# Latent attention with its feed-forward layer: norm two blocks ahead, half a projection in the steps, the window's edge masked on TensorE

## What is computed

```python
q_c = q @ W_dq                                   # q: the normed x, 512 -> 192
q_nope = (q_c @ W_uq); q_rope = rope(q_c @ W_qr) # 16 heads
kv_c = kv @ W_kvc                                # 512 -> 128
k_nope = kv_c @ W_uk; v = kv_c @ W_uv; k_rope = rope(kv_c @ W_kr)
scores = (q_nope . k_nope + q_rope . k_rope) * scale
good = (k_ids <= seg_id) & (k_ids >= seg_id - 8)
scores = where(good, scores, -1e30)
out = softmax(scores) @ v @ W_o
x = x + out
x = x + (silu(ln(x) @ gate * gate_s) * (ln(x) @ up * up_s)) @ down * down_s
```

## Time and profile before

| | us |
|---|---|
| median of the three runs shown (820.82 to 823.79) | 823.74 |
| the profiled execution | 825.13 |
| its span, first to last instruction | 823.2 |
| PE busy in it | 754.3 |
| DVE busy | 461.5 |
| ACT busy | 408.2 |
| POOL busy | 188.3 |
| mean granted clock of PE | 0.955 |
| setup ends at about | 110.5 |
| heads of block 0 begin at | 188 |
| attention ends and the feed-forward layer begins at | 588 |

### The profile page before, as it was taken

How to read it: one execution, slowest core, us unless ns; L and a number is a source line. 1 busy time by engine, 2 the same in 40 slices (tenths; PEclk the granted TensorE clock), 3 DMA queues, 4 the chain that set the end, 5 groups by cost and what they waited for, 6 DMA issues and landing times.

```text
span 823.2 us, 18851 instructions
## 1 busy us (share of the span) xinstructions
PE 754.3 (92%) x7102; PEld 703.3 (85%) x7102; DVE 461.5 (56%) x984; ACT 408.2 (50%) x899; POOL 188.3 (23%) x325
## 2 busy tenths in 40 slices
PE   4899986889999898889899899889999999999997
PEld 4777875769987798779797799778999999999997
DVE  2988763654577345764367545774685263636342
ACT  4788742564446544574355644575588231323231
POOL 2455523433044210533016130422000000000000
PEclk9999996879999899999999899998999999999999
DMA  8899763344322332033320443109120212111021
GB/s 261 260 304 305 248 163 65 80 112 88 71 59 90 78 80 57 26 110 86 66 65 3 123 86 83 34 5 386 65 66 1 59 40 53 43 48 48 15 67 33
DMA packets 46356, 80.89 MB, mean 98 GB/s; under 512 B 5738, under 2 KB 30234, under 8 KB 46282
## 3 DMA queue, kind: packets, MB, share of 16 engines
q1 hardware_dynamic: 40796, 53.34, 25.0%
q0 software_dynamic: 5488, 26.50, 9.4%
HBM read 56.93 MB, written 11.28 MB: 83 GB/s over the span
## 4 chain that ended last, share of the span: by engine, by line
PE 64%; DVE 8%; SPq 5%; issue 3%; ACT 3%; DMA 2%; POOL 1%; DVEq 0%; ACTq 0%; POOLq 0%
PE ps L1335 17%; PE ps L1037 12%; PE ps L907 9%; PE ps L1367 8%; PE ps L1042 6%; SPq L821 5%; PE ps L167 3%; PE ps L980 2%; DVE score L1151 2%; PE ps L953 1%; DVE prob L1175 1%; DMA key_rows<-kv_table,idx 1%; ACT q_lat L1080 1%; PE ps L766 1%; PE ps L1316 1%
## 5 line engine op out<-in xcount | busy, mean ns | idle before, releaser
L1191 DVE TENSOR_TENSOR o_lo<-q_lat,o_hi 128x320 fp32r<-128x320 f32 x80 | 64.6, 813 | 91.0 <-ACT o_hi L1088 88.8
L1037 PE MATMUL ps<-o_hi,wvo_hi 128*128 128x320 f32 x320 | 97.0, 314 | 1.8 <-ACT o_hi L1088 1.8
L1088 ACT ACTIVATE o_hi<-q_lat 128x320 fp32r<-128x320 f32 x80 | 66.9, 842 | 61.1 <-PE ps L1037 60.0
L1037 PE MATMUL ps<-o_hi,wvo_lo 128*128 128x320 f32 x320 | 95.8, 311 | 0.0
L1419 ACT ACTIVATE silu<-ps,ffn_scale 128x320 f32<-128x320 f32 x55 | 29.0, 527 | 97.5 <-PE ps L1335 97.5
L853 POOL TENSOR_TENSOR rot_c<-gathered,cosq 128x192 f32<-128x192 f32 x40 | 27.3, 683 | 213.6 <-PE ps L917 180.1
L1470 DVE SCALAR_TENSOR_TENSOR hidden<-ps,ffn_scale,silu 128x320 f32<-128x320 f32 x55 | 30.2, 549 | 60.5 <-ACT silu L1419 52.9
L1037 PEld LDWEIGHTS ps<-o_hi,wvo_hi 128*128 128x128 f32 x320 | 60.7, 190 | 2.4 <-ACT o_hi L1088 2.1
L1037 PEld LDWEIGHTS ps<-o_hi,wvo_lo 128*128 128x128 f32 x320 | 60.6, 189 | 0.3
L1042 PE MATMUL ps<-o_lo,wvo_hi 128*128 128x320 f32 x320 | 60.4, 310 | 0.0
L487 PE MATMUL ps<-wkv,ctx_hi 128*128 128x384 f32 x192 | 53.4, 388 | 6.4 <-ACT ctx_hi L350 6.4
(11 more groups left out here) (170 smaller groups left out, 1930.6 us busy)
## 6 DMA issues: line engine op xcount, KB each, us to landing
ctx_raw<-ctxT_dram SPq DMA_DIRECT2D x16, 722.0 KB, 7.8
gathered<-key_rows SPq DMA_DIRECT2D x240, 47.2 KB
head_w<-head_w_dram SPq DMA_DIRECT2D x16, 576.0 KB, 5.2
ffn_raw<-ffn_w_dram POOLq DMA_DIRECT2D x11, 768.0 KB, 12.3
kv_table<-tab POOLq DMA_DIRECT2D x16, 288.0 KB, 6.7
rows<-x_dram SPq DMA_DIRECT2D x5, 640.0 KB, 5.2
residual<-x_dram SPq DMA_DIRECT2D x20, 160.0 KB, 2.4
x_rows<-residual SPq DMA_DIRECT2D x20, 160.0 KB, 2.0
```

The source lines that it names most:

```text
L1037: last = pe.matmul(ps[:, 4 + m, 0:TB], w[wt][:, h, cols], o_hi[h % 2][:, :], start=(h == 0 and n == 0), stop=False, skip_group_check=True)
L1088: act.activation(o_hi[h % 2][:, :], q_lat[:, h % 2, :, h // 2], ACT.Copy).then_inc(oh_ok, 1)
L1191: dve.tensor_tensor(o_lo[h % 2][:, :], q_lat[:, h % 2, :, h // 2], o_hi[h % 2][:, :].bitcast(F32), ALU.subtract).then_inc(ol_ok, 1)
```

## The change

- **Norm two blocks ahead.** The norm of block b + 2 is made while the heads of block b run: DVE's pieces behind heads 2 to 9, PE's transposes after heads 10 to 13 (`norm_heads`), ACT's copies beside them. The norm of block 1 is made in block 0: DVE's pieces in its last queries, PE's transposes in its first steps. The norm of the feed-forward layer's block 0 goes into the heads of blocks 3 and 4. SP loads the rows two blocks ahead.
- **Half of the compression earlier.** The first output of `compress` (m = 0) goes to bank 6 in the first steps: two of its products before the third mask, two before the fourth. ACT copies it twice (`take_compressed`), and PE waits for the second copy before the first values. The second output stays after the last values.
- **The edge mask by PE.** The table `edge` and one POOL operation a block (`mask_block`) make a stationary operand for each step; the mask product now adds both masks. L1155 and `neg_all` are gone, and the scale goes into the exponential.
- **The first two gathers of block 0** are issued at the end of the setup by POOL, once the first eight contexts are stored.
- **The loop** holds blocks 1 and 2; block 3 is written out. SP's part is written out whole.

```diff
-def compress(pe, b, m, w, rowsT, ps, ln, qc_mm):
-    pe.wait_ge(ln.hi_ok, Count(NLT)(b, NLT))
-    for c in range(KC):
+def compress(pe, b, m, cs, w, rowsT, bank, ln, qc_mm):
+    if 0 in cs:
+        pe.wait_ge(ln.hi_ok, Count(NLT)(b, NLT))
+    for c in cs:
...
# setup, POOL
                 turns(pool, rope)
+                pool.wait_ge(index_ok, 1)
+                pool.wait_ge(front_in, 16)
+                for i in range(2):
+                    pool.wait_ge(tab_out[i], 16 * (NB // 4))
...
+                for k in range(2):
+                    pool.indirect_dma_start(
+                        out=win[k][:, :], out_offset=None, in_=table,
+                        in_offset=bass.IndirectOffsetOnAxis(ap=w["idx_all"][:, k:k + 1], axis=0),
+                    ).then_inc(win_in[k], 16)
...
+def attention_blocks(eng, body):
+    body(0)
+    with eng.Fori(1, BLOCKS - 2) as b:
+        body(b)
+    body(BLOCKS - 2)
+    body(BLOCKS - 1)
...
# attention, SP
+            if b < BLOCKS - 1:
+                load_rows(b + 2)
+            if b > 0:
+                res.rest(sp, b - 1)
+                res.start(sp, b)
...
# attention, POOL
+        def mask_block(b, first):
+            if not first:
+                pool.wait_ge(s_mm, c16(b - 1, 16))
+            pool.tensor_tensor(
+                masks[:, :, :].rearrange("p s (x r) -> p s x r", r=HH),
+                w["edge"][:, bass.ds(b * STEPS, STEPS), :].unsqueeze(3).to_broadcast([P, STEPS, SPOTS, HH]),
+                w["other"][:, :].rearrange("p (x r) -> p x r", r=HH).unsqueeze(1)
+                .to_broadcast([P, STEPS, SPOTS, HH]), ALU.add).then_inc(mask_ok, 1)
...
             if first:
+                mask_block(0, True)
                 load_index(0)
-                gather(0, 0)
-                gather(0, 1)
                 pool.wait_ge(lone_in, 32)
                 rotate(0, 0, True)
                 rotate(0, 1, True)
                 gather(0, 2)
+                ln.root(pool, 1)
...
                 gather(b + 1, 1)
-                ln.root(pool, b + 1)
                 gather(b + 1, 2)
+            if third:
+                ln_f.root(pool, 0)
+            elif not last:
+                ln.root(pool, b + 2)
...
# attention, PE
+            mask_and_rope(b, 1)
+            latent(b, 1)
+            turn_keys(b, 3)
+            if first:
+                ln.turn(pe, 1, 2, (6, 7))
+                ln.turn(pe, 1, 3, (6, 7))
+            else:
+                compress_main((0, 1))
+            mask_and_rope(b, 2)
+            latent(b, 2)
             turn_probs(b, 0)
+            compress_main(range(KC) if first else (2, 3))
...
-                for t in tiles_at(s):
-                    if last_block:
-                        ln_f.turn(pe, 0, t, (2, 3))
-                    else:
-                        ln.turn(pe, b + 1, t, (2, 3))
-            if not last_block:
+            if not last:
                 pe.wait_ge(s_red, c16(b, 16))
-                compress(pe, b + 1, 0, w, rowsT, ps, ln, qc_mm)
-                compress(pe, b + 1, 1, w, rowsT, ps, ln, qc_mm)
+                compress(pe, b + 1, 1, range(KC), w, rowsT, ps[:, 1, 0:TB], ln, qc_mm)
...
+                if h in norm_heads:
+                    t = norm_heads.index(h)
+                    if last:
+                        ln_f.turn(pe, 0, t, (2, 3))
+                    elif not third:
+                        ln.turn(pe, b + 2, t, (2, 3))
...
# attention, DVE
-            dve.scalar_tensor_tensor(
-                out=sa[:, :, :].rearrange("p (e g) j -> p e (g j)", e=2),
...
+        norm_after = {2: 0, 3: 1, 4: 2, 5: 3, 6: 4, 8: 5, 9: 6}
...
-                if o in stats:
-                    next_norm(b, last, stats.index(o))
+                if first and o >= 11:
+                    ln.piece(dve, 1, (o - 11) // 2, x_in, loads=1)
...
+                if h in norm_after and third:
+                    ln_f.piece(dve, 0, norm_after[h], ffn_x_in)
+                elif h in norm_after and not last:
+                    ln.piece(dve, b + 2, norm_after[h], x_in, loads=b + 2)
```

More of the change, by code:

```diff
@@ L66 @@
 FAR = -2.0 ** 127
+SPOTS = 2 * (GQ + 1)
 MEANS = WIN
@@ L655, in finish, with build_attention @@
             sp.wait_ge(s, 32 * BLOCKS)
-def build_attention(nc, block, ctx, a, w, ffn, ps, ident, table, x1, rows, rowsT, four, ln, ln_f, sums, qc_mm):
+def build_attention(nc, block, ctx, a, w, ffn, ps, ident, table, x1, rows, rowsT, four, ln, ln_f, sums, qc_mm, win,
+                    win_in, four32):
     def sb(name, shape, dt=F32, stack=ctx):
@@ L784, in _, with load_rows @@
     def _(sp):
-        def body(b, first, last):
-            sp.wait_ge(ln.turned, c4(b, NLT))
-            if not last:
-                sp.dma_start(rows[:, :, :], a["x"][bass.ds((b + 1) * TB, TB), :]
+        def load_rows(k):
+            sp.wait_ge(ln.turned, c4(k - 1, NLT))
+            if k < BLOCKS:
+                sp.dma_start(rows[:, :, :], a["x"][k * TB:(k + 1) * TB, :]
                              .rearrange("(t p) d -> p t d", p=LT)).then_inc(x_in, 16)
@@ L982, in values, with body, compress_main @@
             last.then_inc(av_mm, 1)
-        def body(b, first, last_block):
+        def body(b):
+            first, third, last = place(b)
+            def compress_main(cs):
+                if not last:
+                    compress(pe, b + 1, 0, cs, w, rowsT, ps[:, 6, 0:TB], ln, qc_mm)
             pe.wait_ge(qc_lo_ok, c2(b, 2))
+            if not first and not last:
+                pe.wait_ge(ln.hi_ok, c4(b + 1, NLT))
             for o in range(4):
@@ L1018, in body @@
                 if s == 0:
+                    if not last:
+                        pe.wait_ge(qc_full, c1(b, 1))
                     values(b, s)
@@ L1104, in body @@
                 take_latent_keys(b, s)
+                if first:
+                    for t in range(2 * s - 4, 2 * s - 2):
+                        ln.high(act, 1, t, (6, 7))
             take_probs(b, 0)
@@ L1110, in body @@
                     exps(b, s + AHEAD - 1)
+                if s == 0 and not last:
+                    take_compressed(b + 1)
                 if s and s + AHEAD < STEPS:
```

211 lines of the change are left out of this document (118 added, 93 removed).

## The result

The changed kernel takes **800.96 us** (median; 797.89 to 802.26) beside 823.76 us for the kernel before on the same chip: ratio 0.971 [0.965, 0.977]. On another chip it took 804.43 us, ratio 0.975 [0.971, 0.978]. The forecast was 802.3. Its profiled execution took 802.26 us (span 800.6), that of before 825.13 (span 823.2), so 22.9 us less where the sum said 21.4. But the parts of the sum came out otherwise, and the experiments show that two of its reasons were wrong and cancelled others.

What follows compares the result with a forecast made beforehand. PE, busy for 754 of 823 us, was taken as the bound. Terms for block 0, starts, ends, compression, transposes and loop summed to -21.4 us: profiled 825.1 to 803.7, median 802.3; range 795 to 815.

Steps and rivals of the forecast that it cites:

- End of the steps: End of a block's steps: removed DVE work brings the last values 1.3 us earlier; -3.9 in blocks 1 to 3.
- The chain of the new wait in block 0: First mask waits behind third gather (17.8 us after the first spread), POOL's root, two tiles, copy; 137.4 us.
- The transposes: Four tiles between heads 10 to 13, where PE has no gap: +1.5 us in blocks 0, 1, 2 and 4.
- rival B: Heads: PE idles more before them and stays at half clock into two heads per block; +15, 817 us; chance 0.09.
- Block 0: First block in all -7.9 us: -7.3 up to the last values, -2.1 compression, +1.5 transposes.
- Rival A: The first block doesn't start earlier: gather lands no sooner or the new wait eats it; 809 to 810 us; chance 0.14.
- Starts: Start of a block's steps: -0.6 us over blocks 1 to 3, -0.4 in block 4.
- Mask: L1155, 0.27 us mean, leaves DVE's chain 40 times; gives some 0.25 us at a block's start and end.
- The other half at the start: Start of steps: four early compression products fill PE's waits, two of them hidden; -0.2 us in each of blocks 1 to 3.
- Compression: Last values to first head, half left: gains 2.1, 2.3, 2.7 and 2.4 us; -7.4 in blocks 1 to 3.
- Loop: One of two returns goes: -5.0 us, bounds -4.3 and -5.7, or 0 if the written-out code stalls.

## Why the prediction was right, and where it was not

The time was right to 1.3 us, and the sum of the profile to 1.5. That the sum came so near is luck in part: block 0 and the compression gave less than forecast or gave it for another reason, the starts and the loop gave more. The largest part of the change, the norm two blocks ahead, was never undone by itself. The loop (6.1 us) and DVE's step (4.6) were; most of the rest can be the norm's move, but that is inferred from what is left over. Three steps of the prediction held, as far as the profiles tell. *End of the steps*: -3.9 forecast, -4.0 in the first profile of the changed kernel, -2.1 in the second. *The chain of the new wait in block 0*: 17.8 us forecast from SP's start to the third gather, 17.76 measured; 34.5 us to the last values where 35.5 stood. *The transposes* in the heads: 1.6 to 1.8 us a block where 1.5 stood. Of this the transposes are 1.3, by profiles whose heads start at full clock; the rest is rival B in small: the first head of blocks 0 to 3 ran at a mean clock of 0.67 to 0.81 in this profile, at 1.00 before. Block 4 with all behind it lost 2.3 us: 1.3 as above, and 1.0 since the clock stayed at 0.50 for 5.7 us from its first head on instead of 3.3. In the profiles of four of the experiments it stayed there for about as long as before, and the loss is 1.3.

**Block 0**, -7.9 forecast, -3.2 measured. The step that failed is "the first two gathers now go out right there ... so spreads start between 114.1 and 118.4". The gathers went out there, but SP's small DMAs stand behind the end of the setup, and that waited for their landing: SP started at 120.29. The sum's own words had the trap in them: POOL "then waited for the end of the stage". I asked when the gather lands, and not what the stage's end waits for. Rival A had the right place, with another mechanism.

**Starts**, -1.0 forecast (blocks 1 to 4), -4.6 measured. The step "Mask" took L1155 at its mean of 0.27 us. In the first step of a block it takes 0.59 (block 1 before) or 0.75 (put back), beside POOL's rotations, and `prob` is stretched too. The step back alone costs 3.7 us at the four starts. The step "The other half at the start" called the first two early products "hidden" and expected full clock from them: without them the starts of blocks 1 to 3 are 3.2 us shorter in all, and at full clock too. In blocks 1 to 3, then, the step gave 2.2 us, the products took 3.2, and the stretch still fell by 3.0; the step was never put back without the early products, so the two may not add up, and up to 4 us there have no cause shown. The table in section 1, "Specifications", of "GPSIMD Engine Reference" of the Trainium skill says that POOL's way to SBUF is shared with DVE, with contention where a DVE operation has two SBUF inputs. These rows agree: `prob`, with two inputs, takes 0.98 us beside a rotation and 0.22 without. The forecast cited it and said that it "would not change the sum". It did.

**Compression**, -7.4 forecast, -7.5 measured, and this is the right number for the wrong reason. With the compression undivided the end still falls from 22.8 to 18.3 us over blocks 1 to 3, at a clock of 0.73 to 1.00 from the last values to the first head where it was 0.60 to 0.75. What is left by the move is 1.7 to 3.0 us against the two profiles of the changed kernel (2.7 to 8.1 against the six others), and the starts pay 3.2 for it. The faster end, as far as one profile of each can show it (21.6 us in that of the kernel before with block 3 written out), comes from the rest of the change (the norm's work and transposes gone from the last steps, the mask's step gone). With that step put back the ends are 5.52, 5.52 and 5.40 us, as in the changed kernel on that chip (5.52 three times), which speaks for the norm's; the norm's alone was not run. The step that failed is "with one half left: 1.6 us of values + 4.3 us at half clock", set against an end that was itself taken as fixed. Two of its readings were off as well: block 2's first head was taken from a piece of the chain (376.04 us), while PE's timeline has it at

```profile
375.64 0.55 PE L1037 MATMUL ps<-o_hi,wvo_hi 128*128 128x320 f32 x1
```

So that end is 8.1 us and not 8.5, block 3's 6.5 and not 6.9, and the term by its own working is -6.6.

**Loop**, -5.0 forecast, -8.8 measured. The one return taken away gave 6.4 us in the profiles, -6.1 us by itself; the forecast had valued one at 4.3 or 5.7. The rest is that the return left cost 2.0 us instead of 4.4. It is not a gain of the change that can be counted on: with the mask's step put back it cost 6.2, in the other kernels with one return 1.4 to 5.4.

## What to carry to other kernels

Before an asynchronous transfer is moved ahead of a stage's end, see what that end waits for: it may wait for the transfer, and then all engines pay what one queue gains. Put filler work for PE where it waits at the same moment for something long, not at a start that is short of PE time; there it cost 0.4 us at most, and the clock stayed up for what came behind. A DVE step's mean duration is not its price on the path: take the row where it stands beside POOL's work. Look at several executions before a stretch that depends on the clock is compared: the same code took 10.2 to 16.6 us here. And a sum that comes out right has not shown its terms; undo them one by one.

## What the runs showed of the hardware

- The end of the setup waited for POOL's indirect gathers: the other engines stood 6.7 us after the issue of one, 8.9 us after that of the second of two.
- A gather beside SP's rows and residual landed after 10.7 to 13.1 us, all others after 5.4 to 9.0.
- A loop's return cost PE, in waits for nothing but issue, between 1.09 and 4.17 us, and the queries behind the stall 0.1 to 2.3 us more. What sets it stays open. SP's load of 640 KB of rows doesn't by itself: it was issued 2.8 us ahead of a stall of 1.70 us and of one of 3.94, and in the second it had landed 1.9 us before the end. All blocks written out showed no stall.
- POOL's mask operation, 1024 elements bf16, took 1.93 us, where the forecast had estimated 2.9 from the f32 rotations.
- After two waits of some 1.5 us PE's next products ran at the lower of its two levels for part or all of the way in 37 of 40 ends of steps (eight records 4.63 us at 0.50), and at full clock in three, with the same waits. With the waits filled down to 0.22 us they ran at full clock in eight of eight (2.42 us). The Trainium skill, page "TensorE: Matmul & The Clock Gate", section "Loop structure matters more than you think", says that waits between products let the clock fall; 37 of the 40 agree.
